# Where the pieces of a state-space scan stand between three stages of a decoder layer

## The reference, cut to what matters

```
x = x + attn(layernorm(x))                         # 16 heads of 32, causal
x = x + scan_block(ctx, z=layernorm(x))            # per step: state = state*exp(d*A) + (d*u)*b ; y = sum(state*c)
x = x + ffn(layernorm(x))                          # silu(x Wg + g_lora) * (x Wu + u_lora), then Wd; top 2 of 8 experts
```

## Time and profile before

| what | value |
|---|---|
| median of 3 runs | 1601.74 us (1595.86 to 1602.22) |
| the profiled execution's own time | 1596.27 us |
| its span in the trace | 1594.5 us |
| mean granted TensorE clock | 0.888 of full speed |
| busy: PE, DVE, ACT, POOL | 87%, 70%, 43%, 7% of the span |

### The profile page before, as it was taken

One profiled execution on the slowest core, in us unless ns is written; L12 is line 12 of the kernel. 1 busy time (PEld: TensorE's weight loads), 2 busy tenths in 40 slices (PEclk: granted clock), 3 DMA queues, 4 the chain that ended last, 5 costly groups with the idle time before them and its releaser, 6 DMA issues.

```text
span 1594.5 us, 16051 instructions
## 1 busy us (share of the span) xinstructions
PE 1382.6 (87%) x5768; PEld 675.0 (42%) x5768; DVE 1108.9 (70%) x1247; ACT 689.2 (43%) x1501; POOL 112.0 (7%) x116
## 2 busy tenths in 40 slices
PE   6756667999988799899989699899989698799999
PEld 2334334444443355434444255444434255454443
DVE  4899996557989775737999866637998967621120
ACT  6155653344543484343552376361562277321110
POOL 0000001000200000000210000100210000100000
PEclk8955558999999699999999778999999869789999
DMA  4166662114667631113766722002566751101112
GB/s 191 40 152 157 141 142 50 42 50 112 172 145 172 171 68 27 40 35 81 180 147 159 196 67 54 27 32 80 141 150 152 169 139 28 27 19 61 50 35 84
DMA packets 53277, 158.80 MB, mean 100 GB/s; under 512 B 5072, under 2 KB 10704, under 8 KB 44752
## 3 DMA queue, kind: packets, MB, share of 16 engines
q0 software_dynamic: 9216, 67.11, 20.4%
q1 hardware_dynamic: 25664, 54.23, 10.1%
q10 hardware_dynamic: 18320, 36.45, 8.6%
HBM read 86.20 MB, written 4.46 MB: 57 GB/s over the span
## 4 chain that ended last, share of the span: by engine, by line
issue 30%; PE 29%; DVE 26%; DMA 7%; ACT 5%; POOL 2%; ACTq 0%; DVEq 0%; POOLq 0%
DVE state L1082 10%; DMA y_sb<-state 7%; PE ps_a L890 5%; PE ps_a L970 4%; DVE state L1077 4%; PE ps_w L869 3%; DVE state L1087 3%; PE ps_a L816 3%; PE ps_a L902 2%; PE ps_b L830 2%; ACT r L622 2%; POOL rstd L474 2%; DVE neg_max L1117 2%; PE ps_b L910 2%; PE ps_w L778 2%
## 5 line engine op out<-in xcount | busy, mean ns | idle before, releaser
L890 PE MATMUL ps_a<-xt,w_sb 128*128 128x512 f32 x704 | 316.1, 603 | 0.0
L1082 DVE TENSOR_TENSOR_SCAN state<-decay,state 128x2048 f32<-128x2048 f32 x64 | 282.8, 4419 | 7.5 <-ACT decay L580 3.4
L1253 DVE TENSOR_TENSOR r<-r,ps_a 128x512 f32<-128x512 f32 x132 | 88.6, 683 | 206.4 <-ACT r L674 206.4
L816 PE MATMUL ps_a<-r 32*128 32x512 f32 (+3 forms) x512 | 140.6, 634 | 84.0 <-ACT r L622 57.5
L890 PEld LDWEIGHTS ps_a<-xt,w_sb 128*128 128x128 f32 x704 | 135.6, 194 | 171.1 <-issue 171.1
L674 ACT ACTIVATE r<-ps_a 128x512 f32<-128x512 f32 x132 | 78.4, 597 | 297.8 <-PE ps_a L902 158.7
L580 ACT ACTIVATE decay<-dt_sb,decay_rate 128x511 f32<-128x511 f32 x256 | 163.0, 712 | 63.2 <-DVE state L1087 31.2
L622 ACT ACTIVATE r<-ps_a,neg_max 128x128 f32<-128x128 f32 (+3 forms) x256 | 133.8, 534 | 118.7 <-DVE neg_max L1117 118.3
L902 PE MATMUL ps_a<-r,wb_sb 128*128 128x512 f32 x352 | 166.7, 596 | 11.1 <-DVE r L1253 8.9
L970 PE MATMUL ps_a<-wd_sb,r 128*128 128x512 f32 x352 | 161.8, 611 | 0.8 <-DMA wd_sb<-in_w_down 0.8
L1077 DVE TENSOR_TENSOR state<-du_sb,bc_sb 128x2048 f32<-128x2048 f32 x64 | 146.3, 2287 | 5.2 <-DMA y_sb<-state 5.0
(11 more groups left out here) (123 smaller groups left out, 1448.4 us busy)
## 6 DMA issues: line engine op xcount, KB each, us to landing
y_sb<-state POOLq DMA_DIRECT2D x64, 1024.0 KB, 9.7
bc_sb<-bc_rows ACTq DMA_DIRECT2D x64, 512.0 KB, 5.1
w_sb<-in_w_tiles SPq DMA_DIRECT2D x44, 512.0 KB, 4.0
wd_sb<-in_w_down SPq DMA_DIRECT2D x44, 256.0 KB, 3.6
wb_sb<-in_w_adapt SPq DMA_DIRECT2D x44, 128.0 KB, 2.1
xa<-in_x SPq DMA_DIRECT2D x4, 1024.0 KB, 5.2
out_x<-xb SPq DMA_DIRECT2D x16, 256.0 KB, 7.0
xn_att<-in_ctx_t SPq DMA_DIRECT2D x4, 512.0 KB, 6.1
```

Of the source, the lines that this page charges most:

```text
L816: nc.tensor.matmul(score_place(s, k), q_t[rows, m, i * P:(i + 1) * P], k_t[rows, 0:width], start=True, stop=False, tile_position=(rows.sta ...
L890: mm = nc.tensor.matmul(ps_a[:, 2 * (f % 2) + half, :], w_sb[:, slot, at + k * P:at + (k + 1) * P], xt[:, k, :], start=(k == 0), stop=Fals ...
L1082: nc.vector.tensor_tensor_scan(flat, decay[:, n % 2, :, :].rearrange("p j l -> p (j l)"), flat, 0.0, ALU.mult, ALU.add).then_inc(scan_chai ...
```

## The change

`NORM_SLOTS` put one row tile's normalization behind the last evaluation of each of the tiles 5, 6, 7 and 8, with the slot's piece between its first and its second half. `NORM_AT` puts two of them behind evaluation e = 1, which is (0, 1), and two behind e = 4, which is (1, 1), ahead of the pieces there. `IN_EVALS` has 33 pieces in the wide tiles where it had 30: three behind (f, 1), where there were two, in tiles 1 to 3. So the polynomial takes three tiles and not four, and state 0 begins in tile 4. Beside the down products stand 16 pieces where 22 stood, and in attention 11 where 8 stood: one in each odd step but those of the narrowest tile and the last. The first batch's own plan is untouched.

```diff
-NORM_SLOTS = [EVAL_AT[FT - 2 - NT + i, 2] for i in range(NT)]
+NORM_AT = {EVAL_AT[0, 1]: (0, 1), EVAL_AT[1, 1]: (2, 3)}
...
-IN_EVALS = [(0, 2, 1)[k] if e >= POLY_AT and f <= LAST_TILE else 0 for e, (f, k) in enumerate(EVAL)]
-IN_DOWN = 22 
+POLY_TILES = (NPOLY + 2) // 4
+IN_EVALS = [((0, 3, 1) if f <= POLY_TILES else (0, 2, 1))[k] if e >= POLY_AT and f <= LAST_TILE else 0
+            for e, (f, k) in enumerate(EVAL)]
+IN_DOWN = 16
+ATT_PIECES = [s for s in range(STEPS - 1) if s % 2 and s // 2 % NT]
...
-                 spread_over(PIECES - sum(IN_EVALS) - IN_DOWN, STEPS - LAST_STEPS) + [0] * LAST_STEPS)
+                 [int(s in ATT_PIECES) for s in range(STEPS)])
...
-                    inverse_deviation("att", t + 1, [i for i in range(NT) if NORM_SLOTS[i] == e])
+                    inverse_deviation("att", t + 1, NORM_AT.get(e, ()))
...
-                    if e in NORM_SLOTS:
+                    for i in NORM_AT.get(e, ()):
                         dve.wait_ge(loaded["x"], 16 * t + 32)
-                        deviation("att", t + 1, xa, NORM_SLOTS.index(e))
+                        deviation("att", t + 1, xa, i)
+                    for i in NORM_AT.get(e, ()):
+                        scaled("att", t + 1, xa, xn_att, i)
                     for piece in PLAN_NEXT[e]["dve"]:
                         scan_piece(t + 1, piece)
-                    if e in NORM_SLOTS:
-                        scaled("att", t + 1, xa, xn_att, NORM_SLOTS.index(e))
```

## The result

| | before | changed |
|---|---|---|
| median | 1598.95 us (12 runs, 1595.86 to 1605.59) | 1606.45 us (12 runs, 1604.24 to 1609.22) |
| ratio | | 1.0044, 95% interval 1.0034 to 1.0054 |
| own time of the profiled execution | 1596.27 us | 1604.78 us |

The change made the kernel slower by 0.4%, 7 us. I had forecast 11 us less. The measured time lies above my range, and the difference has the other sign.

What follows compares the result with a forecast made beforehand. It took PE to bound the wide tiles, DVE the down products, and a loop attention; +4.9 - 12.5 + 4.0 = -3.6 us per round, three rounds -10.8 us, gave 1591 us, range 1576 to 1606.

Steps and rivals of the forecast that it cites:

- What bounds the stages: Per round: PE nearly full in the wide tiles, DVE late in the down products, nobody full in attention's loop.
- Two normalizations behind (0, 1) cost nothing: Wide tiles: DVE waits 5.35 us there, and two normalizations need 3.6 us, so cost 0.
- The stall in tile 1, 5.9 us: Wide tiles, behind (1, 1): two normalizations 3.6 and one more piece 2.3 us, uncovered, make PE stand; +5.9 us per round.
- Tiles 5 to 8, -2.7 us: Wide tiles: without normalizations, tiles 5 to 8 go at PE's 12.02 us each; gain 2.7 us per round.
- The clock in the wide tiles, 1.7 us: Wide tiles: half clock on PE behind the new stall costs 1.7 us per round, between 0.6 and 2.8.
- Down products, -12.5 us: Down products: six fewer pieces on DVE bring `finish` 12.5 us earlier per round; bounds 9 and 15.4 us.
- Attention, +4.0 us: Attention: three more pieces cost +3.5 us, plus 0.5 for the clock, per round; bounds 0 and 11.5 us.
- Its direct part, +3.5: Attention: what the moved pieces and decay add after waits hide some, summed over groups of eight steps, +3.5 us per round.
- decay 15: Attention: moved from step 4 into step 12, where ACT needs 2.55 us ahead of the next exponentials; +2.4 us paid.
- the 7 us that I had named as a sign of being wrong: Attention: the forecast counts as wrong if attention grows by under 1 or over 7 us.
- Rival 2: Attention pays in full: each piece delays the next maxima, the decay the exponentials; +4.4 us per round, 1615 us; chance 0.10.
- rival 5: Wide tiles: POOL's power takes 2.5 us both times, the stall grows by 3.2 us; -0.4 per round, 1600 us; chance 0.07.

Runs made afterwards that it cites:

- e8: The kernel before with only the four normalizations moved, two behind (0, 1) and two behind (1, 0), all pieces in old slots; ratio to before 0.9949.
- e3: The changed kernel with the second pair of normalizations one evaluation earlier, behind (1, 0) and not (1, 1); ratio to before 0.9939.
- e1: The kernel before with three pieces moved from the down products into attention (19 and 11), wide tiles as before; 1608.8 us, ratio to before 1.0065.
- e2: The changed kernel with 19 pieces beside the down products and 8 in attention in the old steps; ratio to before 0.9984.
- e5: The changed kernel with 10 needless PE products ahead of the scores of attention steps 13, 21 and 29; ratio to before 0.9923.
- e7: e3 with 18 pieces beside the down products and 9 in attention, one in step 5, the last in step 29; 1576.8 us, ratio to before 0.9848.
- e4: The changed kernel with 10 needless PE products behind PE's wait in attention steps 5, 13, 21 and 29; ratio to before 1.0191.
- e11: The kernel before with only 16 needless PE products ahead of each round's first attention scores; ratio to before 1.0029.

## Why the prediction was wrong

By its own steps:

- *What bounds the stages*: right. PE in the wide tiles, DVE in the down products, a loop of all in attention.
- *Two normalizations behind (0, 1) cost nothing*: right (e8; and from evaluation 1 to evaluation 4 it is 20.1 us in both kernels).
- *The stall in tile 1, 5.9 us*: right, the evaluations are 9.95 us apart where I had 10, and PE waits 6.31 us where I had 6.3. e3 took the 3.6 us of the normalizations away again.
- *Tiles 5 to 8, -2.7 us*: right; e8 has it alone, 2.8. In the changed kernel, from evaluation 7 to evaluation 31, it is 2.2.
- *The clock in the wide tiles, 1.7 us*: right, 1.8 from evaluation 4 to evaluation 7. The bounds 0.6 and 2.8 that I gave for it come from no row. The sum of the stage was +5.3 for +4.9.
- *Down products, -12.5 us*: right, -12.5. The move of v was freed, and `finish` is still DVE's. In e1 and e2, however, I expected 9 us of three pieces and got 6.3: the first three pieces of the six are worth as much as the last.
- *Attention, +4.0 us*: this is the step that failed. Its direct part, +3.5 (a `run` for an `out`, two `out` into waits of 1.68 us, decay 15, step 30), holds about: with the clock held up in most of the stage in e5 it is 83.0 us, +3.9, and some 1.2 us of these are low clock that e5 leaves in place (5.6 and 4.1 us on average for the two pairs behind step 13, where 5.2 and 3.3 are reached elsewhere). The failed term is the sentence "with one more `run` that lets PE stand, I add 0.5 for the clock", to which the prediction gives no row. It measured at least 5: +9.1 in all, less 3.9 with the filler. The +9.1 is also over the 7 us that I had named as a sign of being wrong. Three rounds of 5.1 us are 15 of the 19 us by which the profiled execution missed my 1585.5; 1.2 more are in the wide tiles, 1.8 in the part ahead of the rounds.
- *Rival 2*, attention pays in full, had the right sign, and attention passed the 7.6 us from which it decides, but it has neither the size (12.0 with 0.5 for the clock, 9.1 measured) nor the mechanism: DVE's pieces are not paid in full. That it comes nearer to the measured time than the forecast is luck.

Where the reasoning went astray: I put a small number on the clock in attention without reading it from a row. I had rows in which PE stood for 7.0 and 8.3 us and the clock fell behind them, and I used them for the wide tiles and not for attention. There each group of eight steps now has a scan and an `out` in neighbouring odd steps, PE waits some 3 us in the middle of many small products, and the clock falls in every group, where before it was low mostly in the first group and in the last pair. And in attention, unlike the wide tiles, PE at half clock is slow enough to become the one that DVE waits for (12.7 us for 5.3). The sum of small waits says how much can be hidden; it doesn't say that PE may be made to wait.

What stays open: why the low stretch lasts six steps in one attention of e7 and about two in another with the same instructions and the same waits ahead of it. I didn't separate what part the scan has in it and what the `out` behind it has, and no run took decay 15 alone.

## What to carry to other kernels

Where a stage is a loop through several engines and PE is neither the bound nor far from it, price an insertion twice: what it adds to its own engine beyond the wait it fills, and what PE does at half clock for the stretch behind the wait it is given. Work whose result is needed only much later belongs into waits that the trace shows; here the step from one evaluation to the one before it was worth 5.3 us a round. If PE must wait in such a loop, useless products that fill the wait up to its end can be cheaper than the low clock behind it (e5). Behind the wait they cost their own length (e4), and ahead of a wait of which 6.6 us remained they changed nothing (e11).

## What the runs showed of the hardware

The granted clock is part of the result and not of the noise alone: identical instruction lists took 77.8 or 84.8 us with the clock at 0.83 or 0.74 (e7). The clock fell behind a wait of 3.0 us in a stretch of small products (changed kernel, 591.06) and not at the same place behind one of 0.8 us (e5); but it also fell behind waits of 0.4 and 1.5 us (e5, step 13) and behind 0.95 and 0.31 us (e7). So the length of the last wait alone doesn't decide it in these traces. The Trainium skill, "TensorE: Matmul & The Clock Gate", "The HAM clock gate", has it that activity releases the throttle; these runs agree, as products whose results nobody reads raised the clock of an attention from 0.74 to 0.84 and to 0.92. That the release need not come at once is shown by e7, where PE was at half clock for 20.2 us in which it was busy throughout. POOL's power took 2.52 us beside a 128x2048 piece. In tile 1 of the changed kernel, with no such piece beside it, the two behind evaluation 4 took 0.55 and 0.78 us, and DVE waited 0.44 us for the second, which rules rival 5 out:

```profile
710.94 0.55 POOL L477 TENSOR_TENSOR rstd<-var_eps,cst 128x1 f32<-128x1 f32 x1 [18.30 <-DVE var_eps L1023]
712.00 0.78 POOL L477 TENSOR_TENSOR rstd<-var_eps,cst 128x1 f32<-128x1 f32 x1 [0.51 <-DVE var_eps L1023]
```
